# Turning the oldest tile's rows ahead of the values products in the steps of a decoder layer that have no expert work

## The reference, cut to what matters

```
x = layernorm(x + linear_attention(x))      # 16 heads, softmax over channels (q) and over tokens (k)
x = layernorm(x + cross_attention(ctx, x))  # 8 heads, 77 keys per batch, masked
x = layernorm(x + experts(x))               # 8 experts, top 4 per token, gelu, 256 -> 1024 -> 256

logits = einsum(x, router_w); w = softmax(logits); topk(w, 4), renormalized
out = sum_k w_k * (gelu(x @ up_w[e_k]) @ down_w[e_k])
```

## Time and profile before

| what | value |
|---|---|
| time, median of 3 runs | 1265.32 us |
| lowest, highest run | 1259.17, 1267.60 us |
| span of the profiled execution | 1256.1 us |
| PE, PEld busy (share of the span) | 1096.2 us (87%), 904.3 us (72%) |
| DVE, POOL, ACT busy | 764.7 us (61%), 645.5 us (51%), 495.2 us (39%) |
| chain that ended last | PE 65%, DVE 15%, POOL 9%, issue 5% |

### The profile page before, as it was taken

The page is one execution under the profiler, slowest core; times in us unless marked ns, Lnnn a source line. Parts: engine busy times, 40 slices in busy tenths (PEclk is TensorE's granted clock), DMA queues, the critical chain, the costliest instruction groups (busy, mean ns, idle before and its releaser), DMA issues.

```text
span 1256.1 us, 27061 instructions
## 1 busy us (share of the span) xinstructions
PE 1096.2 (87%) x8572; PEld 904.3 (72%) x8572; DVE 764.7 (61%) x1863; ACT 495.2 (39%) x913; POOL 645.5 (51%) x736
## 2 busy tenths in 40 slices
PE   6568977878887699988899999999999999999960
PEld 3345665656655488877788888888888888888750
DVE  2667978987897687754844444444444444444326
ACT  3754534544343255553233333333333333333214
POOL 3012317756673777766775455555555555554324
PEclk9878979979896799998999999999999999999985
DMA  6421223222212333433444654555544445563326
GB/s 176 154 91 59 93 75 104 74 65 80 77 38 64 72 62 76 71 64 68 65 76 77 134 85 77 77 77 77 77 77 77 77 77 77 77 77 60 64 55 243
DMA packets 163039, 105.07 MB, mean 84 GB/s; under 512 B 107596, under 2 KB 153856, under 8 KB 162656
## 3 DMA queue, kind: packets, MB, share of 16 engines
q1 hardware_dynamic: 132896, 67.67, 21.4%
q0 software_dynamic: 30016, 35.68, 19.7%
HBM read 51.91 MB, written 36.04 MB: 70 GB/s over the span
## 4 chain that ended last, share of the span: by engine, by line
PE 65%; DVE 15%; POOL 9%; issue 5%; DMA 3%; ACT 3%; SPq 0%; POOLq 0%; ACTq 0%; DVEq 0%
PE big L1663 25%; PE big L1682 13%; PE trans L1682 11%; PE big L1705 3%; POOL slot_records L779 3%; PE big L1604 2%; PE small L1751 2%; PE small L1615 2%; POOL early_sums L809 2%; PE trans L1533 2%; POOL rstd L755 1%; PE small L1583 1%; PE big L1707 1%; DVE stat L1047 1%; DVE w_down L1043 1%
## 5 line engine op out<-in xcount | busy, mean ns | idle before, releaser
L1663 PE MATMUL big<-xgT,w_up 128*128 128x256 f16 (+1 forms) x3456 | 408.0, 267 | 12.7 <-DMA xgT<-xg 10.1
L1663 PEld LDWEIGHTS big<-xgT,w_up 128*128 x3456 | 324.7, 98 | 55.9 <-issue 16.4
L902 ACT ACTIVATE h<-big,up_scale 128x512 f32<-128x512 f32 x270 | 185.5, 687 | 451.4 <-PE big L1663 437.6
L1296 DVE TENSOR_SCALAR hh<-h,h_scale 128x512 f16<-128x512 f32 x270 | 133.8, 496 | 312.5 <-ACT h L902 310.8
L809 POOL DMA_INDIRECT token_sums<-y,rec x99 | 163.2, 1649 | 244.5 <-ACT y L910 223.5
L1682 PE MATMUL big<-w_down,hh 128*128 x1264 | 216.8, 274 | 2.8 <-DVE hl L1298 2.5
L1298 DVE SCALAR_TENSOR_TENSOR hl<-h,h_scale,hh 128x512 f16<-128x512 f32 x270 | 203.0, 752 | 9.6
L1682 PE MATMUL big<-w_down,hl 128*128 x632 | 173.0, 274 | 0.0
L1682 PE MATMUL trans<-w_down,hh 128*128 x896 | 152.8, 273 | 2.6 <-DVE hl L1298 2.4
L779 POOL DMA_INDIRECT slot_records<-recs,posi x128 | 130.2, 1017 | 35.3 <-issue 33.6
L1682 PEld LDWEIGHTS big<-w_down,hh 128*128 128x128 f16 x1264 | 123.2, 98 | 20.8 <-issue 3.8
(11 more groups left out here) (249 smaller groups left out, 1512.4 us busy)
## 6 DMA issues: line engine op xcount, KB each, us to landing
w_down<-in_L_ffn_up_w_dram SPq DMA_DIRECT2D x8, 1024.0 KB, 5.0
w_down<-in_L_ffn_down_w_dram SPq DMA_DIRECT2D x7, 1024.0 KB, 5.7
XA<-in_x_dram SPq DMA_DIRECT2D x32, 128.0 KB, 2.6
XRES<-in_x_dram SPq DMA_DIRECT2D x32, 128.0 KB, 2.4
token_rows<-XR SPq DMA_DIRECT2D x32, 128.0 KB, 1.8
sums<-token_sums SPq DMA_DIRECT2D x8, 512.0 KB, 7.2
out_dram<-sums SPq DMA_DIRECT2D x8, 512.0 KB, 2.6
xgT<-xg SPq DMA_TRANSPOSE x135
```

The lines of the kernel that those rows point to most:

```text
L902: act.activation(h[:, i % H_RING, :], psu[up_bank(i)], ACT.Gelu_apprx_tanh, scale=k["up_scale"][:, t:t + 1]).then_inc(gelu_ready, 1)
L1296: dve.tensor_scalar(hh[:, i % HALF_RING, :], h[:, i % H_RING, :], k["h_scale"][:, t:t + 1], None, ALU.mult).then_inc(hh_ready, 1)
L1663: ins = pe.matmul(psu[up_bank(i)][:, j * size(t):(j + 1) * size(t)], w[:, ws, c, m:m + P], xgT[:, t % 2, xs * CC + c, 0:size(t)], start=(n ...
```

## The change

In the first loop of PE, the one over steps below 38, `turn_second(c4)` moves from behind `context_values(c3)` to ahead of it. `route(c4)` stays behind the values products. The order of bank uses does not change, and no other engine's order does.

```
                 if c2 is not None:
                     context_logits(c2)
+                if c4 is not None:
+                    turn_second(c4)
                 if c3 is not None:
                     context_values(c3)
                 if c4 is not None:
-                    turn_second(c4)
                     route(c4)
```

## The result

The changed kernel takes 1272.39 us (median of 13 runs, 1268.25 to 1276.64) against 1264.57 us (13 runs, 1258.28 to 1271.99) for the kernel before: a ratio of 1.007, with a 95% interval of 1.0049 to 1.009. That is 7.8 us slower. The forecast was +1.1 us. The measured time lies just inside the forecast's range, 1257.5 to 1272.5, but that is no hit: against the runs of the kernel before, the loss is clear of noise, and it is seven times what was forecast.

A forecast was written before the change was run, and what follows sets the result against it. PE and DVE, both nearly full, were taken to alternate as bound in the changed stretch, PE alone late. Step terms summed to +1.09, say +1.1 us, on the median 1265.32: 1266.4 us, range 1257.5 to 1272.5.

The forecast's parts named there:

- What bounds it: Changed stretch, 120 to 413 us: DVE 85% and PE 83% busy, taking turns; from 590 us PE alone, 93%.
- x2 on time: Steps with the norm ready: path from turn to router 1.40 us instead of 2.02, 0.62 less, the copy hidden beside the values.
- x2 late: Steps where values queue behind the turn's wait for DVE's norm: router 0.15 to 0.88 us later in eight steps.
- X: End of DVE's norm of x2; break-even about 0.6 us after the time at which the values could have started.
- What of each reaches the end: Step-by-step sum of gains and losses that the chain carries to the kernel's end: +1.09 us, say +1.1.
- Steps 14 and 15 together: Router of step 14 0.25 us late, key maximum of step 16 later in turn: +0.15 us.
- rival B: Slower: late turns 3.2 us, state products of three closing steps at the lower clock 5.4; +8.6 us, 1273.9; chance 0.15.
- The gain of step 32: PE 0.62 us ahead, but the key maximum can move up only to the key copy's end: -0.37 us.
- that of step 19: PE's 1.71 us wait for pT hides the turn, router starts earlier, DVE had been idle 0.46: -0.46 us.
- The sum at full clock: Terms of all changed steps added: +1.09 us, say +1.1, giving 1266.4 us.
- Rival A: Gain reaches the end: 12 steps at 0.62 give -7.4 us, 1257.9, chance 0.20; all 21 give 1252.3, chance 0.04.
- Rival C: ACT's copy of the shares or the bank holds the turn in place: 0, 1265.3 us; chance 0.58 shared with the forecast.

The follow-up runs named there:

- e2: Kernel before with the turn moved ahead of the values only in the ten steps where x2 was late; 1268.3 us, ratio to before 1.0051.
- e13: Kernel before with the turn moved ahead of the values in steps 13 and 14 alone; 1264.0 us, ratio to before 1.0011 (0.9982 to 1.0039).
- e8: Kernel before, order kept, with identity transposes filling PE's long waits in steps 17, 26, 35 and 37; 1271.6 us, ratio to before 1.0063.
- e4: Changed kernel plus 99 identity transposes ahead of PE's wait for x2, in 11 steps with long waits; 1264.3 us, ratio to before 1.0011.
- e12: e4 with the turn back behind the values in steps 17, 26, 28 and 35; 1259.5 us, ratio to before 0.9994.
- e1: Kernel before with the turn moved only in the 11 steps where PE hardly waited for x2; 1265.7 us, ratio to before 1.0024.

## Why the prediction was wrong, step by step

**What bounds it** held. The late stretch is unchanged, and the loss of the early one came through whole.

**x2 on time**: the path from turn to router. Predicted 1.40; in step 19 the turn stands at 199.28 and the router at 200.59, 1.31. The waits for the copy x2T fell to 0.9, as forecast (about 1).

**x2 late**: the router's lateness was right in kind, and step 35 has the size (2.51 us from turn to router against 2.64). New waits at the turn were forecast in eight steps, 0.4 to 1.7 us each, 7 to 8 us in all; they are 13, up to 2.4 and 15.3 in all. The mistake: the 0.62 won in one step was counted as a gain or as nothing, and never added to the next step's wait. In step 14 X is 0.83 behind the values' old start, and 0.83 is the pause in e2, without the lead; with PE 0.6 earlier it would be 1.4, and 1.64 was measured.

**What of each reaches the end** is the step that failed. It has +0.15 for "Steps 14 and 15 together", and "steps 20, 21, 29 and 30 stay as they are". These terms price a late turn by its lateness alone. What PE has queued behind the pause was priced at the lower clock only in the closing steps, in rival B. In step 14 it cost 3.5 instead of 0.15 (e13 has the same 3.5), and in step 20 2.4 instead of 0, of which step 22 gave back 0.8. In the changed kernel's profile step 28 has 3.5 instead of 0.49 and step 31 3.0 instead of 0, but there runs with the order of before have nearly as much (e8, 3.3 and 3.1). The gain of step 32 came, -0.5 against -0.37, that of step 19 in part, -0.2 against -0.46.

**The sum at full clock** was not contradicted: e4, with the pauses filled and all else as in the change, is at 1.0011, which is 1.4 us, in an interval from -0.8 to +3.5 us; the terms gave +1.1. Putting the turn back in four of the eight late steps (e12) took off 2.1 us against 1.7, as loosely.

**Rival A** (the gain reaches the end) fell: e1, the steps with x2 on time alone, is slower. **Rival B** had the right mechanism, a longer pause and the lower clock, but at the state products; its chance of 0.15 was too small. That its price of 8.6 us is near the 7.8 measured is luck: of its 5.4 us for the closing steps the profile shows 1.6, in step 26 alone, and not as the change's own. **Rival C** (the turn cannot move) fell with the waits for x2T, 10.9 us to 0.9. Two signs that the prediction named for being wrong came true: the first expert product is over 4 us later, and the state products of step 26 take more than 6.5 us.

**The clock behind a pause.** In the changed kernel the clock falls behind pauses of 1.64, 1.93 and 1.72 us at the turn, where PE had been busy before and was busy after. The Trainium skill (TensorE: Matmul & The Clock Gate, HAM oscillation) describes a failure of this kind: waits between bursts of products bring the throttle back, and the next products start cold. Its example has waits for a DMA of about 3 to 5 us. The traces here agree in kind, with shorter pauses. They do not give a rule by the pause's length: in the kernel before, PE idled 1.71 us ahead of the values of step 19 and the products behind it ran at full clock, while in e1 the clock fell in step 14 behind pauses of 0.60 and 0.47 us. What else decides was not found.

## What to carry to other kernels

Before work of PE is moved behind a wait that another engine ends, add the time that the move wins to the wait that follows: where the other engine sets the pace, as DVE did here, PE's gain comes back as a pause. Then price the pause with what PE has queued behind it at half its clock as well as by its length; in step 14, 1.6 us of pause cost 3.5 us, though not every pause of that length did. A cheap test is to fill the pause with products that nobody reads. If the kernel gets faster and its mean granted clock rises, the clock had its part; but the fill must end before the wait does, or it costs more than it gives. And look at the same step in several profiles before a loss in it is put down to a change.

## What the runs showed of the hardware that was not expected

A single pause of 1.64 us in a stretch where PE was otherwise busy was followed by some 7 us at 1.2 GHz, twice (step 14 of the changed kernel and of e13), while one of 0.83 us at the same place was not (e2). The lower level began 1.0 and 1.2 us after PE had resumed, not in the pause. In step 20 the same split shows in all profiles without a fill: 1.93 or 1.94 us three times with the fall, 1.08 to 1.13 us five times without. Nor is it the same in each execution: the profile of e13 has stretches at the lower level near 302 to 315 and 350 us, which the profile of before has not, in steps that both kernels share. And 99 transposes of added work took back 5.9 of the changed kernel's 7.0 per mille, some 7.4 us.
